# Three edits to a four-layer kernel: a pipelined split of q and k, a last network that takes both halves in one cycle, and norms scaled by ScalarE

## The reference, cut to what matters

```python
x = _layernorm(x + attention(x))   # 16 heads of 8; q, k, v, o are low-rank linear maps amp*cos(phase) @ basis
x = _layernorm(x + ffn(x))         # router to the top 2 of 8 experts with room for 640 tokens each, and one shared expert
x = _layernorm(x + mixer(x))       # short convolution, then a scan h = dA*h + dBu over 1024 steps, 16 states of 256 channels
x = _layernorm(x + cycles(x))

def _layernorm(x, axis=-1, eps=1e-05):
    m = jnp.mean(x, axis=axis, keepdims=True); v = jnp.var(x, axis=axis, keepdims=True)
    return (x - m) / jnp.sqrt(v + eps)

def cycles(x):                                           # the last network
    gf = global_net(x.mean(axis=1, keepdims=True))       # 128 -> 64 -> 32 -> 1, gelu, gelu, sigmoid
    out = x
    for _ in range(3):
        tf = coupling_net(out)                           # 128 -> 128 -> 64 -> 32 -> 1, three gelu, sigmoid
        coupling = 0.1 + adaptive_range * (0.7*gf + 0.3*tf - 0.5) * 2.0
        out = out + coupling * twist(out)                # twist: swaps the two halves of the 128 channels, some signs turned
    return out
```

## Time and profile before

| | us |
|---|---|
| median of 3 runs | 962.42 (960.38 to 962.68) |
| the profiled execution | 961.26 |
| its span | 959.6 |
| busy in the span: TensorE, VectorE, ScalarE, GpSimd | 757.4, 742.0, 470.8, 395.6 |

### The profile page before, as it was taken

One profiled execution on the slowest core, in us unless ns is written; L12 is line 12 of the kernel. 1 busy time (PEld: TensorE's weight loads), 2 busy tenths in 40 slices (PEclk: granted clock), 3 DMA queues, 4 the chain that ended last, 5 costly groups with the idle time before them and its releaser, 6 DMA issues.

```text
span 959.6 us, 12348 instructions
## 1 busy us (share of the span) xinstructions
PE 757.4 (79%) x3664; PEld 301.3 (31%) x3664; DVE 742.0 (77%) x1187; ACT 470.8 (49%) x550; POOL 395.6 (41%) x511
## 2 busy tenths in 40 slices
PE   5369999999999999988669983964667766678783
PEld 3212222222222222245547771321222222225211
DVE  3589999999999999666011225878999999998758
ACT  2237777777777777734213222784323323231452
POOL 3526533322333222005714543008987787570000
PEclk9659999999999999997979996956999989899997
DMA  5652122212222113120124413023544434420131
GB/s 125 203 210 53 53 54 56 53 49 53 55 53 57 50 53 93 44 59 26 52 59 125 120 55 99 3 91 132 198 157 149 153 129 162 147 88 1 44 74 58
DMA packets 57431, 83.79 MB, mean 87 GB/s; under 512 B 16211, under 2 KB 35078, under 8 KB 57382
## 3 DMA queue, kind: packets, MB, share of 16 engines
q1 hardware_dynamic: 44450, 66.19, 22.4%
q0 software_dynamic: 9472, 11.09, 4.0%
q10 hardware_dynamic: 3460, 5.89, 1.7%
HBM read 63.58 MB, written 16.16 MB: 83 GB/s over the span
## 4 chain that ended last, share of the span: by engine, by line
PE 39%; DVE 35%; issue 12%; POOL 5%; DMA 4%; ACT 3%; SPq 1%; DVEq 0%; ACTq 0%; POOLq 0%
DVE arena L1029 13%; PE pair L1436 10%; PE pair L1424 7%; PE pair L1519 7%; DVE arena L1288 7%; DVE arena L1282 5%; PE pair L1625 4%; PE pair L1614 4%; POOL slot_x_d L639 3%; POOL arena L703 1%; DVE xnum L283 1%; DVE ln_stats L271 1%; PE pair L1680 1%; DVE arena L1347 1%; DVE xT L1348 1%
## 5 line engine op out<-in xcount | busy, mean ns | idle before, releaser
L1029 DVE TENSOR_REDUCE arena<-pair 128x1 f32<-128x512 f32 x512 | 327.0, 685 | 20.2 <-PE pair L1426 16.8
L753 ACT ACTIVATE arena<-pair 128x1024 f32<-128x1024 f32 x256 | 248.2, 1021 | 94.9 <-PE pair L1436 94.8
L703 POOL TENSOR_TENSOR arena<-arena 128x1024 f32<-128x1024 f32 x64 | 149.9, 2355 | 47.8 <-DVE arena L1282 43.5
L1282 DVE TENSOR_TENSOR_SCAN arena<-pair,arena 128x1024 f32<-128x1024 f32 x64 | 145.7, 2277 | 2.6 <-POOL arena L703 2.6
L908 ACT ACTIVATE pair<-arena,alog 128x1024 f32<-128x1024 f32 x64 | 71.5, 1118 | 148.8 <-DVE arena L1282 148.8
L1519 PE MATMUL pair<-arena 128*32 128x512 f32 x1024 | 136.8, 606 | 0.6 <-ACT arena L753 0.6
L1738 PE MATMUL pair<-arena,ident 128*128 128x512 f32 x256 | 127.9, 624 | 11.7 <-DVE arena L1294 11.7
L1436 PE MATMUL pair<-arena 99*128 99x512 bf16 x512 | 134.8, 386 | 0.1
L1424 PE MATMUL pair<-arena 64*128 64x512 bf16 x256 | 102.8, 402 | 30.2 <-DVE arena L1029 22.6
L1426 PE MATMUL pair<-arena 64*128 64x512 bf16 x256 | 102.9, 402 | 0.0
L1729 PE MATMUL pair<-arena,sel 96*128 96x512 bf16 x128 | 40.6, 400 | 72.3 <-DVE arena L1288 66.3
(11 more groups left out here) (262 smaller groups left out, 953.5 us busy)
## 6 DMA issues: line engine op xcount, KB each, us to landing
arena<-b_rows_d SPq DMA_DIRECT2D x64, 512.0 KB, 3.6
arena<-in_L_ffn_w SPq DMA_DIRECT2D x16, 256.0 KB, 2.9
arena<-q_parts_d SPq DMA_DIRECT2D x32, 96.0 KB
arena<-q_parts_d POOLq DMA_DIRECT2D x32, 96.0 KB, 2.4
arena<-k_parts_d SPq DMA_DIRECT2D x32, 96.0 KB
arena<-xT SPq DMA_DIRECT2D x12, 256.0 KB
slot_x_d<-zero ACTq DMA_DIRECT2D x4, 645.0 KB, 8.9
arena<-slot_x_d SPq DMA_DIRECT2D x8, 322.5 KB, 4.1
```

The source lines that it names most:

```text
L703: g.tensor_tensor(dBu[:, k % HRING, :], du[:, q, :], Bs[:, k % HRING, :], ALU.mult)\
L753: sc.activation(probs[:, kt % NPROB, :], st_pair[kt % 2][:, :], ACT.Exp, scale=SCALE)\
L1029: v.reduce_max(mx[:, mslot, n // 2, n % 2:n % 2 + 1], ring_bank[item % 3], AX).then_inc(s_("ring_read"), 1)
L1282: v.tensor_tensor_scan(hh[:, k % HRING, :], dA_pair[k % 2][:, :], dBu[:, k % HRING, :], 0.0, ALU.mult, ALU.add)\
```

## The change

1. *Split.* x is loaded in two halves with a semaphore each, the second behind the basis loads, and the turning of the second half comes behind the effective weights. Part 1 of chunk n+1 comes ahead of part 2 of chunk n on ACT, and its residue ahead of part 3 on VectorE. The stores of q and k have semaphores of their own; the first head's loads start with q's three rows, which wait for q's stores alone, then k's.
2. *Norms.* Groups 0 to 2: `ln_end` forms -mean/std, and ACT scales (`ln_apply`). Group 3: as before, on VectorE (`ln_late`).
3. *Experts.* The last expert but one is scattered without the wait for its stores; group 1's first row is summed on VectorE, ACT and POOL keep groups 2 and 3; a square root whose result isn't used stands ahead of the picked rows on ACT.
4. *Network.* Both halves go through the same cycle, in a new order on all engines; the two products of a half come ahead of its two sums; the turning back starts after all.

The diff, cut (the waits of later readers on the new semaphores, `early_ready` for groups 0 to 2 and `late_ready` for group 3, are left out):

```diff
-        def ln_end(dve, v, ch, t0, n, count, ready):
+        def ln_end(dve, v, ch, t0, n, count):
+            dve.wait_ge(s_("ln_sqrt"), count)
+            ch(v.reciprocal(lnv[:, t0:t0 + n, 1], lnv[:, t0:t0 + n, 1]))
+            v.scalar_tensor_tensor(lnb[:, t0:t0 + n], lnv[:, t0:t0 + n, 0], -1.0, lnv[:, t0:t0 + n, 1], ALU.mult, ALU.mult)\
+                .then_inc(s_("ln_scale"), 1)
+        def ln_late(dve, v, ch, t0, n, count):
             dve.wait_ge(s_("ln_sqrt"), count)
             ch(v.reciprocal(lnv[:, t0:t0 + n, 1], lnv[:, t0:t0 + n, 1]))
             for t in range(t0, t0 + n):
+                v.tensor_scalar(xres[:, t, :], xres[:, t, :], lnv[:, t, 0:1], lnv[:, t, 1:2], ALU.subtract, ALU.mult)\
+                    .then_inc(s_("late_ready"), 1)
+        def ln_apply(act, sc, gi, count, ready):
+            act.wait_ge(s_("ln_scale"), count)
+            for t in range(4 * gi, 4 * gi + 4):
+                sc.activation(xres[:, t, :], xres[:, t, :], ACT.Identity, bias=lnb[:, t:t + 1], scale=lnv[:, t, 1:2])\
+                    .then_inc(s_(ready), 1)
...
-            def load_unit(u, slot):
-                for dst, parts, at, ap in (
+            def load_unit(u, slot, first=False):
+                if first:
+                    sp.wait_ge(s_("q_stored"), 3 * 16)
+                for n, (dst, parts, at, ap) in enumerate((
                         (qbuf[0:48, slot, :], q_parts_d, 0, [[L, 2 * HD], [0, 3], [1, L]]),
+                        (qbuf[48:TOP, slot, :], q_parts_d, 2 * HD * L, [[L, HD], [0, 2], [1, L]]),
+                        (qbuf[TOP:ROWS, slot, :], q_parts_d, 2 * HD * L, [[L, HD], [1, L]]),
                         (kbuf[0:48, slot, :], k_parts_d, 0, [[0, 2], [L, 3 * HD], [1, L]]),
...
+                    if first and n == 3:
+                        sp.wait_ge(s_("k_stored"), 16)
...
-            def scatter_expert(i, s):
+            def scatter_expert(i, s, reused=True):
...
-                pool.wait_ge(s_(f"ye_stored{s}"), ST * 16 * (i + 1))
-                pool.sem_inc(s_("ye_left"), 1)
+                if reused:
+                    pool.wait_ge(s_(f"ye_stored{s}"), ST * 16 * (i + 1))
+                    pool.sem_inc(s_("ye_left"), 1)
...
-            scatter_expert(EXP // 2 - 1, 0)
+            scatter_expert(EXP // 2 - 1, 0, False)
...
@@ ScalarE @@
+            part1(0)
+            for n in range(8):
+                if n + 1 < 8:
+                    part1(n + 1)
+                part2(n)
...
@@ VectorE @@
+            residue(0)
+            for n in range(8):
+                if n + 1 < 8:
+                    residue(n + 1)
+                part3(n)
...
             act.wait_ge(s_("mask_ready"), 3)
-            for gi in range(1, 4):
+            sc.activation(rt[:, 5, :], rt[:, 1, :], ACT.Sqrt)
+            for gi in range(2, 4):
+                if gi == 3:
+                    ln_root(act, sc, 0, 5)
...
@@ ScalarE, second norm @@
-            for gi in range(4):
+            for gi in range(1, 4):
+                ln_root(act, sc, gi, 4 + gi + 1)
                 if gi >= 2:
                     copy_x2T(gi - 2)
+                ln_apply(act, sc, gi - 1, 3 + gi, "early_ready")
...
@@ ScalarE, third norm @@
             for gi in range(4):
+                ln_root(act, sc, gi, 8 + gi + 1)
                 if gi >= 2:
                     copy_x3T(gi - 2)
+                if gi > 0:
+                    ln_apply(act, sc, gi - 1, 6 + gi, "early_ready")
...
@@ ScalarE, last network @@
             for i in range(CYCLES):
-                if i > 0:
-                    gelu3(i, 0)
+                gelu1(i, 0, 0)
+                gelu1(i, 0, 1)
                 gelu1(i, 1, 0)
+                if i == 0:
+                    act.wait_ge(s_("mean_ready"), 1)
+                    global_act(0, g1[:, :], bank[5][0:64, 0:B], ACT.Gelu, gb1[:, :])
+                gelu2(i, 0)
...
                 gelu1(i, 1, 1)
+                gelu3(i, 0)
...
+                gelu2(i, 1)
                 tanh(i, 0)
-                gelu2(i, 1)
...
                 gelu3(i, 1)
                 tanh(i, 1)
+            ln_root(act, sc, 0, 13)
+            ln_root(act, sc, 1, 14)
+            ln_apply(act, sc, 0, 10, "early_ready")
+            ln_root(act, sc, 2, 15)
+            ln_apply(act, sc, 1, 11, "early_ready")
+            ln_root(act, sc, 3, 16)
+            ln_apply(act, sc, 2, 12, "early_ready")
...
@@ VectorE, last network @@
-            steady(0, 0)
             for i in range(CYCLES):
+                steady(i, 0)
+                steady(i, 1)
                 update(i, 0)
-                steady(i, 1)
-                if i + 1 < CYCLES:
-                    steady(i + 1, 0)
-                else:
-                    add_back(0)
-                    add_back(1)
                 update(i, 1)
+            for gi in range(2):
+                add_back(gi)
+            for gi in range(2):
+                ln_end(dve, v, ch, 4 * gi, 4, 12 + gi + 1)
             for gi in range(2, 4):
                 add_back(gi)
+            ln_end(dve, v, ch, 8, 4, 15)
+            ln_late(dve, v, ch, 12, 4, 16)
...
@@ TensorE, last network @@
             for i in range(CYCLES):
+                layer1(i, 0, 0)
+                layer1(i, 0, 1)
                 layer1(i, 1, 0)
+                if i == 0:
+                    layer1(i, 1, 1)
+                    global_layer(0, gw[0][:, :], gmean[:, 1, :], bank[5][0:64, 0:B])
+                layer2(i, 0)
+                if i == 0:
+                    global_layer(1, gw[1][:, :], g1[:, :], bank[5][0:32, 0:B])
+                else:
+                    layer1(i, 1, 1)
+                layer3(i, 0)
+                if i == 0:
+                    global_layer(2, gw3b[:, :], g2[:, :], bank[5][:, 0:B])
+                    pe.wait_ge(s_("global_act"), 3)
+                layer2(i, 1)
                 layer4(i, 0)
                 layer3(i, 1)
                 layer4(i, 1)
-            stay_awake(10, bank[7])
+            stay_awake(6, bank[7])
+            for c in range(NCH):
+                back(c)
```

More of the change, by code:

```diff
@@ L783, in _ @@
                 for gi in (2 * b, 2 * b + 1):
-                    act.wait_ge(s_("ln_var"), gi + 1)
-                    sc.activation(lnv[:, 4 * gi:4 * gi + 4, 1], lnv[:, 4 * gi:4 * gi + 4, 1], ACT.Sqrt).then_inc(s_("ln_sqrt"), 1)
+                    ln_root(act, sc, gi, gi + 1)
+                for gi in (2 * b, 2 * b + 1):
+                    if gi < 3:
+                        ln_apply(act, sc, gi, gi + 1, "early_ready")
                 for c in (2 * b, 2 * b + 1):
@@ L989, in _, with copy_xT @@
             v.tensor_scalar(wtmp[:, 0, :], wtmp[:, 2, :], -3.1415925, None, ALU.max).then_inc(s_("args_ready"), 1)
-            for c in range(1, NCH, 2):
+            def copy_xT(c):
                 dve.wait_ge(s_("xT_done"), c + 1)
                 v.tensor_copy(xT[:, c * CH:(c + 1) * CH], bank[c][:, :]).then_inc(s_("xT_copied_v"), 1)
+            copy_xT(1)
             dve.wait_ge(s_("sin_done"), 1)
@@ L1203, in _ @@
                 dve.wait_ge(s_(f"picked{gi}"), 2 * 16)
-                if gi > 0:
-                    dve.wait_ge(s_("first_added"), gi)
-                for w in range(1 if gi > 0 else 0, 2):
+                if gi > 1:
+                    dve.wait_ge(s_("first_added"), gi - 1)
+                for w in range(1 if gi > 1 else 0, 2):
                     for t in range(4 * gi, 4 * gi + 4):
@@ L1377, in _, with x_T @@
             pe.wait_ge(s_("ident_ready"), 1)
-            pe.wait_ge(s_("x_loaded"), 32)
-            for c in range(NCH):
-                for k in range(4):
-                    last = t.transpose(bank[c][:, k * P:(k + 1) * P], xres[:, 4 * c + k, :], ident[:])
-                last.then_inc(s_("xT_done"), 1)
+            def x_T(b):
+                pe.wait_ge(s_(f"x_loaded{b}"), 16)
+                for c in (2 * b, 2 * b + 1):
+                    for k in range(4):
+                        last = t.transpose(bank[c][:, k * P:(k + 1) * P], xres[:, 4 * c + k, :], ident[:])
+                    last.then_inc(s_("xT_done"), 1)
+            x_T(0)
             pe.wait_ge(s_("wcos_ready"), 1)
```

193 lines of the change are left out of this document (89 added, 104 removed).

## The result

The changed kernel takes 953.15 us, the median of five runs (950.39 to 955.99), against 962.2 (five runs, 960.38 to 962.68): ratio 0.9905 [0.9889, 0.9922]. The forecast was 949.5, the range 944.5 to 955.5. The profiled execution took 951.42, its span is 949.8: 9.8 less than before, where 12.85 were forecast. The largest miss is the first norm, 4.15 us worse than its term; 2.0 us that came back in stages which were not edited hide part of it.

What follows compares the result with a forecast made beforehand. Attention (72 to 400 us) has no slack; the edited start, norms and network are serial chains, so time saved there moves all that follows. Terms sum to -12.85 us: 948.4 profiled, 949.5 on the median; range 944.5 to 955.5.

Steps and rivals of the forecast that it cites:

- start: Split of q and k, stores and first head's loads: first score 2.6 us earlier, ends -0.5 and -4.9.
- first norm: First norm with groups 0 to 2 scaled on ACT: +0.15 us, from -0.2 to +0.5.
- network, to the third tanh: Last network in its new order: two periods save 4.3 us; term -4.4, from -2.0 to -5.5.
- end behind it: From the third cycle's tanh to the span's end: 20.85 us instead of 23.65; term -2.8, from -1.5 to -3.3.
- Groups 0 and 1 are hidden: VectorE waits for a transfer of heads behind them.: First norm: scaling these two groups on ACT costs nothing, within the term of +0.15 us.
- rival 5: TensorE's clock stays low longer behind the start: gain gone at 1.3 further heads, up to 970 us with two; chance 0.05.
- k lands near 29.95 (0.45 earlier; I expect no gap before it any more): Start: k's store, issued at 25.42 not 26.42, lands 0.45 us earlier; k's loads go out from 30.35.
- rival 4: Start: the last load lands in 2.9 us; start term -4.9, time 947.3 us; chance 0.10.
- the prediction's estimate of -5.7: Start: by the skill's transfer formula the last small load lands 2.1 us after issue, making the term about -5.7.
- Rival 3: Network: half 1's transfer is late, 0.85 us above the slack, twice; time 951.3 us; chance 0.10.
- none idle for a transfer: Network, sign to look for: one half's bases 12.0 us apart, with no base waiting for its transfer.
- Rival 2: ACT becomes the bound of the norms at 2.3 us per group; total -9.5, time 952.9 us; chance 0.13.

Runs made afterwards that it cites:

- the fourth experiment: The changed kernel with the start undone (split chunk by chunk, q and k loaded together, x loaded whole): 952.68 us, ratio 0.9909.
- the ninth: The changed kernel with VectorE scaling the first norm's groups 0 and 1 and 10 filler matmuls instead of 14 ahead of group 0's transposes: 949.75 us.
- the fifth experiment: The changed kernel run again, not edited: 953.38 us, ratio 0.9890.
- experiments 8: The changed kernel with the first norm wholly on VectorE and five parameter loads moved behind the first heads' loads: 945.8 us, ratio 0.9823.
- 11: The changed kernel with first norm on VectorE, five parameter loads moved, three filler matmuls behind each of the last ten row scatters ahead of the first expert: 948.23 us.
- 2: The changed kernel with the first norm's groups 0 and 1 scaled by VectorE, group 2 still on ACT: 949.91 us, ratio 0.9882.
- the twelfth: The changed kernel with the second, third and last norm scaled by VectorE, the first still on ACT: 954.81 us, ratio 0.9916.
- the third experiment: The kernel before with only the first norm's groups 0 to 2 scaled by ACT: 963.69 us against 961.42, ratio 1.0023.

## Why the prediction was right, and where it wasn't

Right in sign, range and most terms; the sum was 3 us too good. That the time lies well inside the range is partly luck: without the 2.0 us of the stages that weren't edited it would be 955.2, at the range's upper end. Forecast and the pair of profiles (negative is a gain):

| term | forecast | measured |
|---|---|---|
| start | -2.6 | -1.72 at the first score, -2.01 at A |
| first norm (A-B) | +0.15 | +4.30 |
| scatters | -1.85 | -1.85 from the first rows (573.44) to the last scatter (579.88); B-C -1.37 |
| second norm (C-D) | -1.0 | -1.54 |
| third norm (F-G) | -0.35 | -0.61 |
| network, to the third tanh | -4.4 | -4.16 |
| end behind it | -2.8 | -2.39 |
| not edited: D-E, E-F | 0 | -1.47, -0.55 |

*The step that failed* is "Groups 0 and 1 are hidden: VectorE waits for a transfer of heads behind them." VectorE was hidden, and ACT's four took 1.65 as forecast (1.64); but TensorE stands behind these groups too, with transposes, logits and fillers in front of the spread that the path needs. I looked at whose time the scaling takes and not at who waits in the meantime. By the fourth experiment the wait alone costs little; what costs is the clock behind it. An order of TensorE's work with the spread ahead of these transposes wasn't tried. With ACT scaling groups 0 and 1 and no more fillers, the spread ran at 3.78 in six of seven profiles (all but the fourth experiment); with VectorE scaling them at 1.99 in five of five, the ninth's single pause among them. That is 3.6 to 4.4 us of A-B (2.0 in the fifth experiment, where it fell later). What makes the clock fall behind these pauses and not behind those of the ninth stays open: it is likely there, not certain. The Trainium skill, TensorE: Matmul & The Clock Gate, section on the HAM clock gate, says that the window in which the gate watches TensorE runs freely, so that the same kernel comes out differently from run to run; the changed kernel and its repetition agree, with A-B 28.04 and 26.48. I had the clock only as rival 5, behind the start, where nothing of the kind came.

*Group 2* came out a little dearer than its +0.15 (+0.5 at the end of its range): with it on VectorE A-B is 24.20 and 23.90 (experiments 8, 11), on ACT 24.46 and 24.89 (2, 9).

*The start* is right as a size at the first score. The pair of profiles shows 0.9 less since q landed in 4.37 here; but over the profiles, the old start gives 39.77, 40.34 and 40.23, and the new one with its loads in place 36.55 to 38.05: 2.65 between the means. In the twelfth the q and k loads go out at 28.30 and 30.35, the forecast's numbers. In the whole time the start's gain isn't shown: the fourth experiment, without it, is no slower.

One step of this term failed: "k lands near 29.95 (0.45 earlier; I expect no gap before it any more)". k's store did go out 1.0 earlier, but landed at 31.1 (25.43 and 5.7), where it landed at 30.4 before; in the twelfth experiment it took 4.8 and landed at 30.3. So of the 1.0 us that the earlier store was to use of the faster split, at most 0.1 reached k's landing. What the profiles show as gain is that q's loads no longer wait for k, and a shorter last load: 4.3 to 5.1 us in the eleven profiles with the new order, 5.2 to 6.0 in the three with the old. That refutes rival 4, which had 2.9. The 2.9 for q's third store was a median of three: this store alone took 3.3 in the kernel before.

The fixed 2.0 us plus bytes of the Trainium skill (DMA: Bandwidth & Descriptors, anatomy of one DMA) is stated there for transfers that GpSimd issues. SP issues the last load, and it shared the DMA engines with others, so neither its 5.12 us nor the prediction's estimate of -5.7 bears on that figure.

*The network* and *the end* were worked out from one cycle and came within about 0.4. Rival 3 is refuted: the base waits for its transfer, 1.1 to 1.9 us (so the sign "none idle for a transfer" was wrong), but its product waits for ACT. Rival 2 is refuted by 1.65 and by the twelfth experiment. In the first norm VectorE was the better place for the scaling, and that through TensorE; in the other three ACT's scaling paid 3.4 in the stages (the twelfth experiment). The rule of the Trainium skill for adds and multiplies (ScalarE: Activation LUTs, rules for kernel authors) agrees with the first norm alone.

*The stages that weren't edited* gained 2.0 in this pair, which hid part of the loss. D-E is 40.0 to 41.0 in eleven profiles and 42.2 to 42.4 in three, the kernel before and experiments 8 and 11. These three are just the kernels in which VectorE scales the whole first norm; in the third experiment, where only that norm moved to ACT, D-E fell by 1.65. Whether the one brings the other, or chance does, no run settles; if it does, the first norm on ACT gave back some of what it cost.

## What to carry to other kernels

When work is moved to an idle engine because the busy one has better to do, follow its consumers too: here a scaling 0.5 us longer per group added 1.0 us of pauses, and in six of seven profiles TensorE's clock fell behind them, which cost 2.0 to 4.4 us. Before a chain is shortened, look at the queue that ships its result: here five small loads in front of the stores held the first score back by 3.7 us, more than the whole new start gained (1.7 to 2.7). With one profile per kernel, compare stage by stage, and look at the stages that no edit touches before you believe the total.

## What the runs showed of the hardware

- The clock's level at one place varies between executions of much the same code: the spread took 1.99 behind pauses of 1.32 and 0.88 us in one kernel and 3.78 in six. The first expert's first product took 4.75 us or, where it began low, 6.25 to 7.1; B-C is 138.4 to 138.8 or 140.2 to 141.8 in the kernels with the scatter edit.
- With ten more matmuls an instruction transfer of 0.02 MB started 1.1 us behind A, where it starts 6.05 and 5.76 behind in the same kernels without them; in both kernels where it met the stores of the last head, SP's load of them went out 1.8 to 1.9 us later.
- A 0.5 KB load on SP's queue, the last in front of q's stores, landed 2.6 us after its issue in three profiles and 3.3 in seven. q's first store behind it landed after 2.9 to 3.0 us in the same three and 3.5 in the same seven; with the load moved away it took 2.9 to 3.0 in four of four.
